# Destination stage of a fused graph kernel: the second MLP product moves to the end of TensorE's step

## What is computed

```python
feat = jnp.concatenate([x, out1, out2, out3, u[batch]], axis=1)
h = jax.nn.relu(feat @ W1 + b1)
out = h @ W2 + b2
return out + x
...
x = _layernorm(x + _L1_gnn_ref(x, edge_index, edge_attr_48, L1_gnn_u, batch0, L1_gnn_W1, L1_gnn_b1, L1_gnn_W2, L1_gnn_b2), axis=-1)
```

## Time and profile before

| | us |
|---|---|
| median of 3 runs | 8919.86 |
| lowest, highest | 8855.19, 8929.37 |
| the profiled execution | 8913.22 |
| its span, first to last instruction | 8911.1 |

### The profile page before, as it was taken

The page is one execution under the profiler, slowest core; times in us unless marked ns, Lnnn a source line. Parts: engine busy times, 40 slices in busy tenths (PEclk is TensorE's granted clock), DMA queues, the critical chain, the costliest instruction groups (busy, mean ns, idle before and its releaser), DMA issues.

```text
span 8911.1 us, 104580 instructions
## 1 busy us (share of the span) xinstructions
PE 5383.5 (60%) x26540; PEld 3576.5 (40%) x26540; DVE 4581.9 (51%) x8429; ACT 2765.5 (31%) x5600; POOL 4784.5 (54%) x4823
## 2 busy tenths in 40 slices
PE   1177677777788688888878888867666721111111
PEld 0144455555555466666654444433333310000000
DVE  8644355556566466666653333368777732222222
ACT  0033333334444233333332222246666620000000
POOL 0266444443466455555535555546665566767666
PEclk9988888889899799999989999977777755555555
DMA  0122344445577566666654444433333331212111
GB/s 20 20 65 65 82 138 133 136 136 160 166 224 220 163 200 195 190 196 190 192 157 139 137 137 138 135 90 102 95 92 89 90 61 58 62 56 59 59 57 51
DMA packets 873389, 1059.36 MB, mean 119 GB/s; under 512 B 144448, under 2 KB 507852, under 8 KB 873154
## 3 DMA queue, kind: packets, MB, share of 16 engines
q1 hardware_dynamic: 719654, 806.47, 29.7%
q0 software_dynamic: 153600, 251.49, 11.3%
HBM read 613.72 MB, written 455.71 MB: 120 GB/s over the span
## 4 chain that ended last, share of the span: by engine, by line
issue 24%; PE 21%; another core or an unknown queue 19%; DVE 19%; ACT 9%; DVEq 3%; POOL 2%; DMA 1%; SPq 0%; ACTq 0%; POOLq 0%
PE bank L969 5%; PE bank L955 4%; PE bank L871 4%; ACT mbuf L1112 2%; DVE x L1696 2%; PE bank L919 2%; DVE t L1757 2%; DVE ln2vr L1684 2%; DVE ln3vr L1684 1%; DVE zT L1725 1%; PE bank L1007 1%; PE bank L925 1%; ACT x L1142 1%; DVE ln1vr L1684 1%
## 5 line engine op out<-in xcount | busy, mean ns | idle before, releaser
L871 PE MATMUL bank<-ident,gat 128*128 128x128 f32 x2400 | 457.3, 322 | 1490.2 <-issue 765.2
L1112 ACT ACTIVATE mbuf<-t 128x512 f32<-128x512 f32 x500 | 315.2, 630 | 2946.8 <-DVE t L1757 1134.0
L955 PE MATMUL bank<-x1T,W1x 128*128 128x512 f32 x1600 | 1013.7, 753 | 195.8 <-ACT x1T L1104 132.0
L871 PEld LDWEIGHTS bank<-ident,gat 128*128 128x128 f32 x2400 | 317.1, 166 | 1642.1 <-issue 1443.7
L969 PE MATMUL bank<-W2s,hT 128*128 128x128 f32 x6400 | 888.2, 296 | 1.3 <-issue 1.3
L969 PEld LDWEIGHTS bank<-W2s,hT 128*128 128x128 f32 x6400 | 808.6, 205 | 101.3 <-issue 101.3
L653 POOL DMA_INDIRECT gat<-in_x_rows,pays x400 | 386.4, 966 | 739.8 <-PE bank L871 629.4
L653 POOL DMA_INDIRECT gat<-Z2E,pays x400 | 378.7, 947 | 612.8 <-PE bank L871 444.9
L679 POOL DMA_INDIRECT pays<-PAY,s_q x400 | 385.2, 963 | 580.9 <-DMA PAY<-payl 341.5
L871 PE MATMUL bank<-ident,x 128*128 128x128 f32 x3200 | 540.9, 296 | 227.7 <-DVE x L1696 162.0
L653 POOL DMA_INDIRECT gat<-X,d_x x400 | 401.6, 1004 | 512.7 <-issue 435.2
(11 more groups left out here) (347 smaller groups left out, 12318.5 us busy)
## 6 DMA issues: line engine op xcount, KB each, us to landing
X<-x SPq DMA_DIRECT2D x700, 256.0 KB
fB<-row_s_same SPq DMA_DIRECT2D x400, 256.0 KB
xT<-in_x_fm SPq DMA_DIRECT2D x200, 256.0 KB
out_rows<-x SPq DMA_DIRECT2D x200, 256.0 KB
ffB<-rows_last_notlast SPq DMA_DIRECT2D x100, 512.0 KB
Z1T<-zT SPq DMA_DIRECT2D x100, 256.0 KB
Z1E<-zE SPq DMA_DIRECT2D x100, 256.0 KB
Z2T<-zT SPq DMA_DIRECT2D x100, 256.0 KB
```

The source lines that it names most:

```text
L871: mm = pe.transpose(dst[:, t, :], tiles[t], ident[:, :])
L955: mm = pe.matmul(bH[h][:, :, :], W1x[:, cols], x1T[s][:, :], start=True, stop=kind != "d")
L1112: act.activation(sq[k % 3][s % 2], [bT1, t2[s], bSK, t2[s]][k][:, :, :], ACT.Square).then_inc(S(f"squared{k}", s), 1)
```

## The change

The order of three lists in the destination stage. PE does the second product last in its step instead of second, and the first layer second instead of last. ACT does the relu right behind the copy, ahead of square and root. DVE does the scan `x2_carry` ahead of `layer2`. Lags, waits, tiles and instructions are the same; POOL's and SP's lists are untouched.

```diff
-            steps(pe, EI, (of("d", chain_b1), 0), (of("d", chain_c), 2), (of("d", chain_d1), 3),
-                  (of("d", chain_b2), 1))
+            steps(pe, EI, (of("d", chain_b1), 0), (of("d", chain_b2), 1), (of("d", chain_d1), 3),
+                  (of("d", chain_c), 2))
...
-            steps(act, EI, (x1_out("d"), 0), (square("d", 1), 2), (std("d", 1), 2), (relu("d"), 1))
+            steps(act, EI, (x1_out("d"), 0), (relu("d"), 1), (square("d", 1), 2), (std("d", 1), 2))
...
-            steps(dve, EI, (x2_select, 3), (layer2("d"), 2), (x2_carry, 3), (power("d", 1), 2), (norm2("d"), 2))
+            steps(dve, EI, (x2_select, 3), (x2_carry, 3), (layer2("d"), 2), (power("d", 1), 2), (norm2("d"), 2))
```

## The result

| | before | after |
|---|---|---|
| median of 20 runs, us | 8920.35 | 8865.89 |
| ratio to before, 95% interval | | 0.9949 (0.9929 to 0.9968) |
| span of the profiled execution, us | 8911.1 | 8908.5 |

The change gains 0.51%, 28 to 63 us by the interval, where 120 were forecast. The two profiled spans don't show it: the executions of either kernel spread over about 100 us, and the stages that the change doesn't touch moved as well. The destination stage does show it. From the first to the last start of its scan L1824 it took 5826.56 - 4658.18 = 1168.4 us before and 5797.97 - 4694.71 = 1103.3 us after, 11.80 and 11.14 us a step.

A forecast was written before the change was run, and what follows sets the result against it. PE's waits before the second product were taken to bound the destination stage; afterwards a 9.56 us loop plus late notices gives 10.6 us a step. 97 x (11.83 - 10.6) = 119 us less, 8800 us, range 8670 to 8925.

The forecast's parts named there:

- The relu off PE's path: Destination stage, second product: PE's 0.77 us idle for the relu goes in every step, leaving 9.13 us of own work.
- Late relu notices covered: Destination stage: a relu notice 7.3 us late is covered by 8.3 us of other PE work before the product.
- The loop: Two-step round of gather, turn, first layer, second turn, product, `layer2`, POOL restart: 19.11 us, 9.56 a step.
- The notice of 1.95 us: Loop term: PE's notice to DVE, from the turn's shown end to L1818's start, 1.95 us.
- Late notices: 7.3 us in 17 of 93 steps persist, adding 0.69 to 1.38 us a step: 10.25 to 10.94, taken as 10.6.
- The scan ahead of `layer2`: DVE: select and scan, 1.97 us, fit beside the 2.20 us product; costs nothing, at most 1.28 us where uncovered.
- POOL's 8.5 us as a floor below 9.13: POOL's issues of gathers and scatters take 8.5 us a group, a floor under the step below PE's 9.13.
- SP at 0: SP's list waits for the norm, some 4 us later; its attribute loads are due later still, so priced at 0.
- No gain: Rival: POOL's round with `layer2` sets the pace, the wait moves to the turn, step 11.6 to 11.9 us; chance 0.23.
- Slower: Rival: gather needing up to 13.93 us makes 13.26 us a step, 9059 us; more than 1% slower, chance 0.15.
- All waits gone: Rival: PE continuous at 9.13 to 9.5 us a step, 226 to 262 us less, 8660 to 8695; chance 0.12.
- The signs named in advance: About 104 L1824 scans in 1100 us, L969 near 2.05 us, PE idle 1 to 1.5 us before the turn, POOL about 2.

The follow-up runs named there:

- scat_early_new: Changed kernel with all 253 index-table scatters moved from the destination stage into the first edge stage; 9.28 us a step, ratio 0.9947 to the kernel before.
- scat_half: Changed kernel with 100 of the 253 scatters moved from the destination stage into the first edge stage; 9.73 us a step, ratio 0.9891 to the kernel before.
- pe_only: Kernel before with TensorE's order alone changed, ScalarE's and VectorE's kept; 16.11 us a step, ratio 1.0544 to the kernel before.

## Why the prediction missed

*The relu off PE's path: right.* L925 has no idle time. PE's own work without disturbance is 836.99 / (850 / 9.28) = 9.14 us a step in scat_early_new; 9.13 was forecast.

*Late relu notices covered: right for the product, but the lateness was taken from the wrong number.* Eleven late notices cost nothing before L925. Before the first layer, which waits for the relu of the group before, there were 29.6 us. The 7.3 us of the prediction are ScalarE's idle time; from PE's last row it was 6.2 us before, and 4.7 after.

*The loop: right in sum, two terms wrong.* Forecast 6.52 + 9.13 + 1.95 + 0.68 + 0.83 = 19.11 for two steps. Undisturbed, in scat_early_new, it is 7.62 (gather) + 9.14 + 0.09 (notice) + 1.49 (`layer2` and restart) + 0.21 = 18.55, 9.28 a step. The notice of 1.95 us was taken for ordinary and was already a late one, of the 44 at `x2_select`; that the sum came near is luck, one term too dear and one too cheap. The Trainium skill ("Perfetto Trace Analysis", on the TensorE instruction in the per-instruction lifecycle) says that the shown end is an estimate and that the semaphore goes out later; where nothing disturbs, the two are 0.09 us apart here, so that rule doesn't carry the 1.95. The gather was too cheap, 6.52 from another stage; the estimate from the same skill ("DMA: Bandwidth & Descriptors", anatomy of one DMA on the gpsimd path) gave 6.1, further off still.

*Late notices: the step that failed.* I added 0.69 to 1.38 us to 9.56 and took 10.6, 1.04 us a step for lateness. In the changed kernel they and what follows cost 11.14 - 9.28 = 1.86 us a step, and the gain is 99 x (11.80 - 11.14) = 65 us in the stage instead of 97 x (11.83 - 10.6) = 119. In the old order lateness cost 11.80 - 10.19 = 1.61 us by the same reckoning, so the new order relieved nothing of it. Forecast were 9.90 - 9.56 = 0.34 us from the loop and 0.89 from less lateness; what came was 10.19 - 9.28 = 0.91 from the order and 1.61 - 1.86 = -0.25 from lateness. These differences are taken over chips; on 8689, near the 8678 of scat_early_new, the changed kernel has 11.19. Two things were left out. First, the time that PE waits is not all: PE's idle time is (1100 - 955.87)/99 = 1.46 us a step, 1.32 more than the 0.14 of scat_early_new (13.0 us in 91.6 steps), and its busy time is 955.87/99 = 9.66, 0.52 more than 9.14, at a mean granted clock of 0.93 against 1.00. Second, I took the lateness as partly hidden by the new order and did not look where else PE's notices were late. Before, `x2_select` had 44 late ones, and `layer2` stood behind it, but the gather then had 14.11 us to its turn, where 7.82 are enough when nothing disturbs, and this hid them. Now 19 come late at `layer2`, whose end lets the gather start, and the gather has 9.01 us. Further, `layer2` to gather is 2.12 us where it is 1.49 without scatters: the gather stands behind them on POOL. A shorter step also packs POOL's work closer (603.74 to 663.39 us busy in 1100), and scat_half shows that the price rises steeply with its DMAs; how much of the 1.86 us that makes was not measured.

*The scan ahead of `layer2`: wrong.* It was priced at nothing, because I looked for who waits on DVE and not for the load that the scan releases on SP. By the one chip with both it carries 43 of 76 us. The 76 are the whole gain there, 7416.70 - 7340.46. So a term put at nothing helped; if it is worth as much on the chip of the result, which was not measured, it made the shortfall smaller.

*POOL's 8.5 us as a floor below 9.13: true as a floor, and misleading on chips with late notices.* There the price starts before the floor is reached: POOL still idles 328.9 us before its gathers in 1100, 3.3 us a group. SP at 0 wasn't tested apart from the above.

*The rivals.* "No gain" expected 11.6 to 11.9 us a step and the wait moved to the turn. Half of it came: 100.8 us before the turn, and 11.14 to 11.23 us a step in three profiles. "Slower" wanted 11.07 us from the gather's start to its turn; the mean was 9.0, waiting included. "All waits gone" is what scat_early_new shows, once the scatters are elsewhere. The signs named in advance: 99 scans instead of 104; L969 at 285 ns, near its full-clock 281; PE idle 1.46 us a step where 1 to 1.5 was said, but not before the turn alone; POOL idle 3.3 us a group before the gathers where 2 was said.

**What stays open.** What in the chip holds a notice of PE back, for 1.6 to 7.7 us in `before` and `after`, while many indirect DMAs are issued. Two of the five chips of the experiments showed no remote wait in this stage in any kernel run there, and one of them ran the changed kernel with all its scatters at 9.48 us a step. POOL was busy 596.04 us of 800 there, a larger share than on the chips with late notices:

```profile
3700.00:4500.00 800.00, 775.49 (x3105) 394.80 (x3105) 354.74 (x504) 226.23 (x420) 596.04 (x554) 1.00 0.62 172
```

So a full POOL alone doesn't make a notice late. The other three chips, and the chip of the first result, showed them with the scatters in place, in every kernel but pe_only; scat_half, with fewer, had one. Whether that is the chip itself or what else used it at the time, no run tells. How much of VectorE's 43 us there is on a chip with late notices wasn't measured.

## What to carry to other kernels

Before an idle engine's wait is booked as gain, look where the same lateness will land in the new order; here its source was untouched and it showed up at the next place without cover, with a low TensorE clock behind it. List every late notice of the engine, the harmless ones too: the 44 that cost nothing before were the warning. When an instruction moves, price also what it releases on the DMA queues, and beside which transfer that falls. A stage crowded with indirect DMAs is worth thinning where notices come late: on the chip 8689 moving 100 of 253 small scatters out of this stage took 67 us more off the kernel, where the change of order had taken 30.

## What the chip showed that was not expected

- The same kernel took 7417 us on two chips and 8678 to 8920 us on the others, up to 20% apart, while the change is 0.4 to 1%. Compare only what shared a chip.
- On chips with late notices the first 1.53 small scatters a step cost 0.45 us and the next one 1.46. All 2.53 cost 1.91 us a step, and 1.48 or 1.62 with reads of 16 or writes of 512 bytes a row in their place. As many fills of 0.96 us cost 0.13 us a step (9.41 against 9.28, over two chips).
- After waits of 3.7 and 5.56 us TensorE ran at a granted 0.50; a first layer took 10.3 us instead of 5.8.
